# Flamingo layer with gated attention and mixture of experts: probabilities times values in plain fp32 on 32-column strips instead of a three-pass split product

## The reference

```python
# x: (2, 2048, 512), ctx: (2, 128, 256)
n  = layernorm(x)
qh = heads(n @ Wq + bq); kh = heads(ctx @ Wk + bk); vh = heads(ctx @ Wv + bv)   # 16 heads of 32
attn = softmax(einsum('bhqd,bhkd->bhqk', qh, kh) / sqrt(32))
out  = einsum('bhqk,bhkd->bhqd', attn, vh)            # <- the product that is changed
x = x + tanh(g_xattn) * (concat(out) @ Wo + bo)
f = layernorm(layernorm(x)) * gamma + beta            # router, top 2 of 8 experts, capacity 1280
x = x + tanh(g_ffn) * moe(f)
```

## Time and profile before

| what | value |
|---|---|
| median of 3 timed runs | 2752.97 us (2751.85 to 2756.25) |
| the profiled execution: its span, the only time that its page gives for it | 2753.4 us |
| first stage, from the first instruction to the experts' first transpose | about 579 us |
| one block of the first stage, in steady state | 31.2 us |
| PE busy | 2662.1 us (97%) |
| DVE, ACT, POOL busy | 51%, 36%, 15% |
| mean granted clock of TensorE | 0.983 |

### The profile page before, as it was taken

One profiled execution on the slowest core, in us unless ns is written; L12 is line 12 of the kernel. 1 busy time (PEld: TensorE's weight loads), 2 busy tenths in 40 slices (PEclk: granted clock), 3 DMA queues, 4 the chain that ended last, 5 costly groups with the idle time before them and its releaser, 6 DMA issues.

```text
span 2753.4 us, 41258 instructions
## 1 busy us (share of the span) xinstructions
PE 2662.1 (97%) x14422; PEld 2396.4 (87%) x14423; DVE 1397.1 (51%) x2725; ACT 980.9 (36%) x2543; POOL 420.6 (15%) x395
## 2 busy tenths in 40 slices
PE   6999999959999999999999999999999999999988
PEld 4888888859999888888888888888888999989987
DVE  5787777734444444444444444454444444445555
ACT  4766666522223322232222322232222322232343
POOL 4445455420000100010000200010000200020030
PEclk8999999969999999999999999999999999999999
DMA  7522222232112310132110421131100510133242
GB/s 263 202 79 83 78 94 80 88 117 85 46 46 51 91 46 23 46 71 75 46 36 32 84 86 53 61 70 65 46 33 36 121 46 29 39 79 123 76 125 80
DMA packets 60035, 208.40 MB, mean 76 GB/s; under 512 B 9564, under 2 KB 9836, under 8 KB 51602
## 3 DMA queue, kind: packets, MB, share of 16 engines
q1 hardware_dynamic: 43282, 175.30, 17.8%
q0 software_dynamic: 16640, 31.69, 6.0%
HBM read 145.60 MB, written 67.70 MB: 77 GB/s over the span
## 4 chain that ended last, share of the span: by engine, by line
PE 76%; issue 2%; DVE 1%; ACT 0%; DMA 0%; DVEq 0%; POOL 0%; ACTq 0%; POOLq 0%
PE bank L1549 75%; PE bank L1555 1%; DVE yacc L1489 0%; DVE slotsT_lo L1458 0%; DVE h L1509 0%; ACT slotsT_hi L1381 0%; DMA xrow<-expert_rows 0%; ACT later_hi L1377 0%; ACT yout L1405 0%; ACT h_hi L1419 0%; POOL out_dram L1363 0%; DVE w_lo L1452 0%; DVE early_lo L1452 0%; DVE later_lo L1452 0%; DVEq L1488 0%
## 5 line engine op out<-in xcount | busy, mean ns | idle before, releaser
L1509 DVE TENSOR_TENSOR h<-silu,bank 128x384 f32<-128x384 f32 (+2 forms) x320 | 183.9, 575 | 827.3 <-PE bank L1549 818.3
L1549 PE MATMUL bank<-slotsT_hi,early_hi 128*128 128x384 f32 (+2 forms) x1280 | 445.2, 348 | 13.9 <-issue 9.9
L1549 PE MATMUL bank<-slotsT_hi,w_hi 128*128 128x384 f32 (+2 forms) x1280 | 442.1, 345 | 5.1 <-DVE w_lo L1452 5.1
L1549 PE MATMUL bank<-slotsT_lo,early_hi 128*128 128x384 f32 (+2 forms) x1280 | 443.1, 346 | 0.0
L1549 PE MATMUL bank<-slotsT_hi,early_lo 128*128 128x384 f32 (+2 forms) x1280 | 442.3, 346 | 0.3 <-issue 0.3
L1549 PE MATMUL bank<-slotsT_lo,w_hi 128*128 128x384 f32 (+2 forms) x1280 | 441.8, 345 | 0.0
L1549 PE MATMUL bank<-slotsT_hi,w_lo 128*128 128x384 f32 (+2 forms) x1280 | 440.8, 344 | 0.0
L1419 ACT CAST h_hi<-h 128x384 fp32r<-128x384 f32 (+2 forms) x320 | 169.3, 529 | 741.0 <-DVE h L1509 741.0
L1413 ACT ACTIVATE silu<-bank 128x384 f32<-128x384 f32 (+2 forms) x320 | 162.5, 508 | 722.6 <-PE bank L1549 722.1
L1489 DVE TENSOR_TENSOR yacc<-bank,yacc 128x512 f32<-128x512 f32 x464 | 316.6, 688 | 167.6 <-PE bank L1549 167.6
L1549 PE MATMUL bank<-later_hi,h_hi 128*128 128x512 f32 x1008 | 399.7, 397 | 0.3 <-DVE yacc L1489 0.3
(11 more groups left out here) (212 smaller groups left out, 3908.9 us busy)
## 6 DMA issues: line engine op xcount, KB each, us to landing
staged<-in_moe_w_dram SPq DMA_DIRECT2D x33, 1536.0 KB
raw<-in_moe_w_dram SPq DMA_DIRECT2D x32, 1536.0 KB
xrow<-expert_rows SPq DMA_DIRECT2D x42, 520.0 KB, 9.0
expert_rows<-zeros SPq DMA_DIRECT2D x40, 520.0 KB, 7.7
xin<-in_x_dram SPq DMA_DIRECT2D x17, 512.0 KB, 3.7
xres<-in_x_dram SPq DMA_DIRECT2D x15, 512.0 KB, 3.7
out_dram<-xres SPq DMA_DIRECT2D x15, 512.0 KB
staged<-in_L_xattn_Wq_dram SPq DMA_DIRECT2D x1, 1024.0 KB, 10.6
```

Source lines behind the costliest of these rows:

```text
L1509: nc.vector.tensor_tensor(h32[q % 2][:, 0:W], silu[q % 2][:, 0:W], UB[q % 2][:, 0:W], ALU.mult)\
L1549: last = nc.tensor.matmul(out_ap, st, mv, start=(at == 0), stop=(at == n - 1))
```

## The change

`v_hi` and `v_lo` with their zeros are gone. `vals[b]` holds the values as they are, 16 heads of 32 columns. `heads` does one plain fp32 matmul per head: stationary 128 by 32, moving 128 by 256, written to the partitions `DK * hh` to `DK * (hh + 1)` of the bank; in the built program these carry a tile of 128 rows by 32 columns at column 0, 32, 64 or 96 of the array. The turned probabilities aren't split any more: ACT copies the first token half of a group to `pT`, DVE the second, and neither waits for the other.

```diff
-            v_hi, v_lo = ([t] + [sb(f"v_{h}{b}", [P, H, P], f32r) for b in range(1, B)]
-                          for h, t in (("hi", later_hi), ("lo", later_lo)))
+            vals = [sb(f"vals{b}", [P, H, DK]) for b in range(B)]
...
-            pT_hi, pT_lo = (sb(f"pT_{h}", [P, H, TB], f32r) for h in ("hi", "lo"))
+            pT = sb("pT", [P, H, TB])
...
-                    for parts in (k_hi + k_lo, v_hi + v_lo):
-                        for t in parts:
-                            last = nc.gpsimd.memset(t[:, :, :].bitcast(fp32), 0.0)
-                        last.then_inc(prep_pool, 1)
-                        if parts[0] is k_hi[0]:
-                            rstd_x(0)
+                    for t in k_hi + k_lo:
+                        last = nc.gpsimd.memset(t[:, :, :].bitcast(fp32), 0.0)
+                    last.then_inc(prep_pool, 1)
+                    rstd_x(0)
...
-                    def pT_halves(blk, g):
-                        for t in range(2):
-                            act.wait_ge(pt_ready, 2 * KD * blk + 2 * g + t + 1)
-                            nc.scalar.copy(pT_hi[:, HG * g:HG * (g + 1), t * P:(t + 1) * P],
-                                           PT_BANK[t][:, :].rearrange("p (h t) -> p h t", h=HG)).then_inc(pt_hi, 1)
+                    def pT_first(blk, g):
+                        act.wait_ge(pt_ready, 2 * KD * blk + 2 * g + 1)
+                        nc.scalar.copy(pT[:, HG * g:HG * (g + 1), 0:P],
+                                       PT_BANK[0][:, :].rearrange("p (h t) -> p h t", h=HG)).then_inc(pt_first, 1)
...
-                        for b in range(B):
-                            for hh in range(HG):
-                                last = nc.vector.tensor_copy(mine(v_hi[b], hh), vals(b, hh))
-                        last.then_inc(prep_split, 1)
-                        dve.wait_ge(prep_split, 2)
-                        for b in range(B):
-                            for hh in range(HG):
-                                last = nc.vector.tensor_tensor(mine(v_lo[b], hh), vals(b, hh),
-                                                               mine(v_hi[b], hh).bitcast(fp32), ALU.subtract)
+                        for b in range(B):
+                            last = nc.vector.tensor_copy(vals[b][:, :, :], bank[2 + b][:, :].rearrange("p (h d) -> p h d", h=H))
...
-                    def pT_rest(blk, g):
-                        for t in range(2):
-                            heads, cols = slice(HG * g, HG * (g + 1)), slice(t * P, (t + 1) * P)
-                            dve.wait_ge(pt_hi, 2 * KD * blk + 2 * g + t + 1)
-                            nc.vector.tensor_tensor(pT_lo[:, heads, cols], PT_BANK[t][:, :].rearrange("p (h t) -> p h t", h=HG),
-                                                    pT_hi[:, heads, cols].bitcast(fp32), ALU.subtract).then_inc(pt_lo, 1)
+                    def pT_second(blk, g):
+                        dve.wait_ge(pt_ready, 2 * KD * blk + 2 * g + 2)
+                        nc.vector.tensor_copy(pT[:, HG * g:HG * (g + 1), P:TB],
+                                              PT_BANK[1][:, :].rearrange("p (h t) -> p h t", h=HG)).then_inc(pt_second, 1)
...
-                                pe.wait_ge(pt_lo, at - 1)
+                                pe.wait_ge((pt_first, pt_second)[t], KD * blk + g)
...
-                        pe.wait_ge(pt_lo, 2 * KD * blk + 4 * i + 4)
+                        pe.wait_ge(pt_first, KD * blk + 2 * i + 2)
+                        pe.wait_ge(pt_second, KD * blk + 2 * i + 2)
                         for gg in range(2):
-                            g = 2 * i + gg
-                            last = passes(v_bank(blk, i)[:, gg * TB:(gg + 1) * TB],
-                                          [((v_hi[b][:, h, :], v_lo[b][:, h, :]), (pT_hi[:, h, :], pT_lo[:, h, :]))
-                                           for h in range(HG * g, HG * (g + 1))])
+                            for hh in range(HG):
+                                h = HG * (2 * i + gg) + hh
+                                last = nc.tensor.matmul(v_bank(blk, i)[DK * hh:DK * (hh + 1), gg * TB:(gg + 1) * TB],
+                                                        vals[b][:, h, :], pT[:, h, :], start=True, stop=True)
```

More of the change, by code:

```diff
@@ L187, in flamingo_gated_layer @@
             rs_ready, pn_ready = sem("rs_ready"), sem("pn_ready")
-            pt_ready, pt_hi, pt_lo = sem("pt_ready"), sem("pt_hi"), sem("pt_lo")
+            pt_ready, pt_first, pt_second = sem("pt_ready"), sem("pt_first"), sem("pt_second")
             v_ready, a_hi, a_lo = sem("v_ready"), sem("a_hi"), sem("a_lo")
@@ L538, in step @@
                                 if has(n, -1):
-                                    pT_halves(n - 1, 2)
+                                    pT_first(n - 1, 2)
                                 if has(n, 1) and not (isinstance(n, int) and n == 0):
@@ L547, in step @@
                                 if has(n, -1):
-                                    pT_halves(n - 1, 3)
+                                    pT_first(n - 1, 3)
                             if slot_no == 3:
@@ L555, in step @@
                                 if has(n, 0):
-                                    pT_halves(n, 0)
+                                    pT_first(n, 0)
                                 if has(n, -2):
@@ L562, in step @@
                                 if has(n, 0):
-                                    pT_halves(n, 1)
+                                    pT_first(n, 1)
                                 if has(n, -2):
@@ L568, in _ @@
                     exps(LAST, 2 * KD - 1)
-                    pT_halves(LAST, 2)
+                    pT_first(LAST, 2)
                     a_halves(LAST, 0)
-                    pT_halves(LAST, 3)
+                    pT_first(LAST, 3)
                     a_halves(LAST, 1)
@@ L840, in step @@
                                 if has(n, -1):
-                                    pT_rest(n - 1, 2)
+                                    pT_second(n - 1, 2)
                                     recips(n - 1, 3)
@@ L851, in step @@
                                 if has(n, -1):
-                                    pT_rest(n - 1, 3)
+                                    pT_second(n - 1, 3)
                             if slot_no == 3:
@@ L862, in step @@
                                     recips(n, 1)
-                                    pT_rest(n, 0)
+                                    pT_second(n, 0)
                             if slot_no == 5:
@@ L874, in step @@
                                 if has(n, 0):
-                                    pT_rest(n, 1)
+                                    pT_second(n, 1)
                             if slot_no == 7:
@@ L887, in _ @@
                     x1(LAST - 1, 1)
-                    pT_rest(LAST, 2)
+                    pT_second(LAST, 2)
                     tail_stats(LAST - 1, (0, 1))
-                    pT_rest(LAST, 3)
+                    pT_second(LAST, 3)
                     a_rest(LAST, 0)
```

3 lines of the change are left out of this document (removed).

## The result

The changed kernel takes **2731.82 us** (median of 4 runs, 2727.61 to 2732.53), 21 us less than before. The ratio is 0.9917, with a 95% interval of 0.990 to 0.993: faster by more than the 0.2% that a measurement can tell. The forecast was 2736 us. The profiled execution has a span of 2730.8 us (before 2753.4), so 22.6 us can be looked for in its trace.

The account below looks back on a forecast made before the run. PE's own throughput was taken as the bound (97% busy). 15 x (0.65 + 0.73) = 20.7, 22.3 with the tail, less 5.6 for clock falls: 16.7 us off 2753.4, median 0.4 lower, so 2736 us; range 2723 to 2768.

Parts of the forecast that it names:

- The time of the call: `heads`: 9 steps of 0.228 us, 2.05, plus 0.23 for tile switching, gives 2.28 us per call instead of 2.93.
- The second of head 0 waits for the first; the first of head 1, next in order, can run beside it: `heads`: in program order only neighbouring heads' instructions overlap, one 0.228 us step per head and one at the end.
- full overlap: Rival: all four strips run together, 0.91 us per call, slot 0 gain capped at 1.05; 2727 us, chance 0.10.
- no overlap: Rival: a call's eight matmuls run one after another, 3.64 us, 3.87 with switching; 2766 us, chance 0.15.
- The switch between tile widths: Around `heads`: going into a narrower tile and out again costs 0.23 us per call.
- Slot 0: First `heads` call of a block: 0.65 us shorter, with at most 1.05 before PE waits for POOL's `norm`.
- Slots 2 to 5: From the second `heads` call to the router: gain of 0.73 us per block, not more however short `heads` gets.
- The wait for the turned probabilities: Slot 3, ahead of `heads`: 0.64 of the 0.71 us lost to `pT_lo` would be gone.
- the stall at `rows`: Slot 4, ahead of `turn_rows`: PE's stall moves there from `pT_lo`, about 1 us.
- I redo DVE's list from 260.36, where `q_rest` has ended: DVE, slots 2 to 4: list recomputed from that time, copy ending at 260.96 and `rows` 0.48 us earlier, at 266.11.
- The clock: TensorE's clock in steady blocks: eight falls to 0.50 instead of four, 1.4 us each, 5.6 us lost.
- The tail: After the last steps: `rows`, the last `heads` and the last block's statistics follow about 1.6 us earlier.

Follow-up runs that it names:

- run 4: Changed kernel with the eight matmuls of a call reordered so each strip comes twice in a row (0, 0, 1, 1 ...): 2732.31 us, ratio 0.9905.
- run 1: Changed kernel with each head's values back in a zero-padded 128-column stationary tile, plain fp32, unsplit copies kept: 2755.17 us, ratio 0.9994.
- run 5: Changed kernel with all eight products of a call on the first 32 partitions; output and routing differ: 2730.12 us, whole time not comparable.
- run 3: Changed kernel with all 16 steps written out, no loop on any engine: 2732.02 us, ratio 0.9895.
- run 12: The kernel before the change with its 16 steps written out, none in a loop: 2767.49 us, ratio 1.005.
- run 8: Changed kernel with POOL's four scatter transfers moved behind the block's last `norm` instead of ahead of it: 2789.88 us, ratio 1.0137.
- run 7: Changed kernel with the first half of the next block's queries moved ahead of the row transposes in PE's slot 4: 2698.55 us, ratio 0.9801.
- runs 5 to 10: Six looped variants of the changed kernel; those not named singly: queries first plus later scatters, 2715.18 us; queries first plus x's transposes ahead in slot 2, 2696.78 us.
- run 6: Changed kernel with heads 0 and 2 of a group on the first strip, 1 and 3 on the second; routing differs: 2822.36 us, not comparable.

## Why the prediction was right, and which of its steps were not

**The sum was right, and several of its terms were wrong in directions that cancelled.** Forecast were 2736 us and a block of 29.8. Measured are 2731.8 us, but a looped block takes 30.5. That the whole came within 4 us was in part luck.

**The time of the call: the mechanism was the wrong one.** The step that failed reads "The second of head 0 waits for the first; the first of head 1, next in order, can run beside it". It rests on "PE starts instructions in program order", took that for a limit on overlap and gave 2.28 us. Run 4 shows four strips starting together against the program's order. Measured are 1.00 us, 1.02 with each strip twice in a row (run 4), 1.85 with two strips, 3.57 with one. Four strips each do their own four instructions, about 0.91 us in all, as the *full overlap* rival had it. The estimate 3.64 for no overlap was within 2% of the one-strip run. The switch between tile widths, taken from L1035 as 0.23 us, can't be read so simply. `probs_T` in slot 0 stands 0.97 us apart from `heads` instead of 0.79, and the S behind a call takes 0.80 instead of 0.69. But run 1, which has no narrow tile, shows 0.87 and 0.88 at these places, so much of both goes with the plain fp32 product and not with the width. What the narrow tile adds shows best at the end of a call: from the last instruction's start to the S it is 0.31 us in run 5 and 0.03 in run 1.

**Slot 0: capped as said.** PE could come 1.05 us earlier and then wait for POOL's `norm`; with the call at 1.00 us that bound was reached, the wait of 0.49 us is there, and slot 0 gained 1.0 us. The forecast of 0.65 was too low because the call was put at 2.28 us. It was 1.28 us shorter than that, of which the bound let about 0.4 through.

**Slots 2 to 5: the sign failed in the loops.** The forecast was a gain of 0.73 us, "and not more however short `heads` gets". In the written-out steps it was 0.6 (`probs_T` in slot 2 to the router, 9.46 us before, 8.87 after). In the looped ones they got 0.37 us *slower*. The wait for the turned probabilities, which should have gone, is still 0.85 us, and the stall at `rows` is 1.5 us instead of 1. The step that failed is the sentence "I redo DVE's list from 260.36, where `q_rest` has ended": it took that time as fixed to slot 2, but everything ahead of it on ACT and DVE hangs on `maxima` in slot 1, and that comes 3.0 us behind its S in the looped steps. Written out (run 3) the lateness and the wait for the copy are gone, the stall at `rows` stays at 1.5 us, and the block takes 29.5 us, near the 29.8 forecast. A sign of it stood in the old trace: ACT has 5.4 us of the same "remote" idle time in four blocks (1.3 to 1.4 us in nine of the ten looped steps, and also in step 14, the first behind the second loop). In run 12 it is gone, and it had cost nothing.

**The clock: wrong, on the safe side.** Eight falls were forecast for the steps, two came, where there had been four: a gain of about 3 us and no loss of 5.6. The number isn't fixed by the kernel's waits: run 4, with the same ones, has none in steps 3 to 14. A stall of 1.5 us ahead of `turn_rows` mostly did not bring the clock down; waits of 2.6 to 5.4 us in one slot did, in run 8. That `heads` now fills only strips of the array was no reason either.

**The tail** was to gain 1.6 us and gained 0.5. A fall of the clock (517.0 to 520.4 us) stands in it that the kernel before doesn't have there; how much of the missing 1.1 us that is was not separated. The ends of the pipeline gained more than the forecast gave them: 8.6 us up to step 2 and 3.5 in step 15, where it had 1.38 for each step.

Put together: nine looped steps at 0.7 us, two written-out ones at 1.7, 0.4 lost in the first looped step, 1.4 by the clock, 8.6 and 3.5 at the ends: 22.8, and the trace has 22.7. The forecast had 22.3 of structure and took 5.6 off for the clock.

**What the change is worth depends on what stands around it.** In the given order it is 21 us. In the order of run 7 it is 2747.8 - 2698.6 = 49 us, near the 52 us that PE works less. Most of the missing 28 us are two of the three waits of the first fence: in steps 3 to 14 the one for the copy adds up to 7.7 us and the one for `rows` to 17.8. The third, for `norm`, is still there in run 7.

**Left open** is why ACT and DVE come late in looped steps, and why not in runs 5 to 10, which are looped too. In run 6 PE is later by 0.85 us in slot 0; in run 7 the step has another order. The trace of the changed kernel shows no instruction fetch at the place (none between 323.8 and 448.4 us, with four late steps). It was settled only that it goes when the steps are written out (run 3), that it comes and goes with the spacing and order of the work, and what it costs: about 1 us per block.

## What to carry to other kernels

An engine that gets faster needs its list looked at again: after a change that shortens one engine's work, read the waits that are new, and move ready work in front of the longest of them. Here that was worth more than the change itself. Moving the producer is not the same as moving the consumer: the transfers that were put later to free a `norm` cost 58 us, since their landing was what the next stage waited for.

When work on tiles narrower than the array is priced, price it by how many different tiles are in flight, not by the order of the instructions. And an experiment that alters what reaches the router can't be timed as a whole, since the work behind the router changes with it.

## What the runs showed of the hardware

- Plain fp32 matmuls with a stationary tile of 128 by 32, 256 columns moving, eight to a call: 3.57 us on one strip, 1.85 on two, 1.00 on four, the same for strips in turn and for each strip twice in a row (1.02). Four strips start within 0.04 us of each other, against the program's order too (run 4).
- One of the two instructions of such a matmul takes 0.216 us from start to start, on one strip (run 5) and on the full width (run 1) alike. From the last one to the f32r S it is 0.31 us behind narrow tiles and 0.03 at full width, which makes calls of 3.57 and 3.27 us; the S then takes 0.80 and 0.88 us where it takes 0.69 behind f32r.
- In looped steps DVE can stand idle for 2.0 us, and ACT for 1.0 to 1.4 us (changed kernel and kernel before), with nothing in the trace to account for it. The same kernel written out has no such time on DVE, and on ACT only once, in step 15.
- A program with 16 steps written out instead of five and two loops fetches more instructions, and PE had two idle times of 7.4 us in the experts' stage for which no engine is named, each with a granted clock of 0.50 for 10.2 us; the time won in the attention stage was gone.
- With 2.6 to 5.4 us of waiting within a slot TensorE's granted clock fell to 0.50, in 12 of 12 blocks of run 8. With a single wait of 1.5 us in that slot it mostly stayed at 1.00: it fell in 2 of 12 blocks of the changed kernel and in none of run 4.
